# The squared norm of the second layer norm's vectors, from ScalarE row sums to TensorE column sums

## The reference, cut to what matters

```
x = mobius_add(residual, expmap0(attn_t))
residual = x
xn = layer_norm(logmap0(x))
xm = expmap0(xn * (1 + sc_mlp) + sh_mlp)
ff = plin(plin(xm, w_f1, b_f1), w_f2, b_f2)      # plin(x,w,b) = expmap0(logmap0(x) @ w + b)
```

## Time and profile before

| what | value |
|---|---|
| median of 3 runs | 459.88 us (459.84 to 459.92) |
| the profiled execution: its own time | 458.45 us |
| the profiled execution: span from first to last instruction | 456.3 us |
| TensorE busy | 371.9 us, 81% of the span |
| VectorE busy | 302.3 us, 66% |
| ScalarE busy | 231.8 us, 51% |
| GpSimd busy | 75.1 us, 16% |
| mean granted TensorE clock | 0.938 of full speed |

### The profile page before, as it was taken

How to read it: one execution, slowest core, us unless ns; L and a number is a source line. 1 busy time by engine, 2 the same in 40 slices (tenths; PEclk the granted TensorE clock), 3 DMA queues, 4 the chain that set the end, 5 groups by cost and what they waited for, 6 DMA issues and landing times.

```text
span 456.3 us, 14117 instructions
## 1 busy us (share of the span) xinstructions
PE 371.9 (81%) x5296; PEld 252.8 (55%) x5296; DVE 302.3 (66%) x1938; ACT 231.8 (51%) x1026; POOL 75.1 (16%) x149
## 2 busy tenths in 40 slices
PE   3998999798758897857998999979599889868833
PEld 2655675576646665646666766636344446447411
DVE  5454444675878776787776776653832388699883
ACT  2224422225435324436446455645688888954952
POOL 4000000121000021000022000042200125265580
PEclk9999999999999999999999999985759999995966
DMA  6301910010000000000000000000000000000102
GB/s 177 67 2 38 210 37 1 2 41 11 1 1 3 3 2 1 2 2 1 2 3 3 1 4 1 2 2 4 1 2 3 1 3 3 1 2 1 24 1 69
DMA packets 9561, 8.42 MB, mean 18 GB/s; under 512 B 1275, under 2 KB 8205, under 8 KB 9494
## 3 DMA queue, kind: packets, MB, share of 16 engines
q1 hardware_dynamic: 8950, 7.26, 7.1%
q10 hardware_dynamic: 544, 0.26, 0.2%
HBM read 6.45 MB, written 1.08 MB: 16 GB/s over the span
## 4 chain that ended last, share of the span: by engine, by line
PE 55%; DVE 22%; ACT 12%; issue 5%; POOL 4%; DMA 1%; SPq 0%; DVEq 0%; ACTq 0%; POOLq 0%
PE zb L805 21%; PE tb L928 6%; PE zb L784 4%; DVE prod_hi L1575 4%; PE tb L751 3%; ACT state L1270 3%; PE firsts L1099 2%; PE firsts L984 2%; PE tb L899 2%; ACT prd L1427 2%; PE firsts L968 2%; ACT state L1273 2%; PE zb L790 2%; PE zb L1079 2%; PE firsts L805 1%
## 5 line engine op out<-in xcount | busy, mean ns | idle before, releaser
L805 PEld LDWEIGHTS zb<-prod_hi,whh 128*128 128x128 f16 x1920 | 73.5, 106 | 89.5 <-DVE prod_hi L1575 85.4
L1270 ACT ACTIVATE state<-zb 128x8 f32<-128x8 f32 x240 | 42.7, 178 | 151.9 <-PE zb L805 151.5
L805 PE MATMUL zb<-prod_hi,whh 128*128 128x8 f16 x1920 | 90.8, 171 | 34.4 <-DVE prod_hi L1575 33.7
L1575 DVE SCALAR_TENSOR_TENSOR prod_hi<-state 128x16 f16<-128x16 f32 x255 | 44.6, 175 | 81.9 <-ACT state L1273 79.0
L805 PE MATMUL zb<-prod_lo,whh 128*128 128x8 f16 x960 | 63.2, 172 | 0.0
L1581 DVE TENSOR_TENSOR prod_lo<-prod,prod_hi 128x16 f16<-128x16 f32 x255 | 44.7, 175 | 8.7
L1427 ACT ACTIVATE prd<-zb 128x640 f32<-128x640 f32 x64 | 42.0, 710 | 5.0 <-PE zb L1079 4.3
L805 PEld LDWEIGHTS zb<-prod_lo,whh 128*128 128x128 f16 x960 | 44.0, 106 | 0.9
L1577 DVE SCALAR_TENSOR_TENSOR prod<-state 128x16 f32<-128x16 f32 x256 | 43.2, 169 | 0.3 <-ACT state L1273 0.3
L1273 ACT ACTIVATE state<-zb 128x16 f32<-128x16 f32 x240 | 42.8, 178 | 0.0
L1583 DVE SCALAR_TENSOR_TENSOR state<-prod 128x8 f32<-128x8 f32 x256 | 40.8, 159 | 0.0
(11 more groups left out here) (377 smaller groups left out, 697.2 us busy)
## 6 DMA issues: line engine op xcount, KB each, us to landing
mod<-ada_rows SPq DMA_DIRECT2D x4, 768.0 KB, 11.4
resid<-in_x_dram SPq DMA_DIRECT2D x6, 128.0 KB, 2.9
ffz<-shift_rows SPq DMA_DIRECT2D x4, 131.0 KB, 3.2
out_dram<-state SPq DMA_DIRECT2D x8, 64.0 KB, 2.1
out_dram<-early SPq DMA_DIRECT2D x8, 64.0 KB, 2.1
yy<-in_L_cond_w_ada_dram SPq DMA_DIRECT2D x1, 384.0 KB
early<-in_L_cond_weight_dram SPq DMA_DIRECT2D x2, 128.0 KB
resid<-in_x_dram ACTq DMA_DIRECT2D x2, 128.0 KB, 3.4
```

The lines of the kernel that those rows point to most:

```text
L805: i = pe.matmul(z_bank(t, k)[:, NB * (t % CH):NB * (t % CH) + NB], whh[:, half, p, k, :], src[:, NB * p:NB * p + NB], start=False, stop=Fa ...
L1270: act.activation(r[:, 24:32], z_bank(t, 1)[:, k:k + NB], ACT.Tanh, scale=-1.0 / ZS)
L1575: dve.scalar_tensor_tensor(prod_hi[:, :], r[:, 16:32], 1.0, r[:, 0:16], ALU.add, ALU.mult).then_inc(hi_ready, 1)
```

## The change

The four row sums on ScalarE go. In their place ScalarE makes one square of the transposed copy `T_OT[j]` (128x512, into `T_F[j]`), and TensorE multiplies each 128x128 tile of it with two columns of ones (`ones2`): four more matmuls of 128x2, into two columns that were free in the bank of t6. They stand behind the g products, and `t6_ps` is raised only behind them. VectorE's copy takes four values instead of three for each tile; its first step of `usum` reads the norm from that copy and no longer waits for `v_sq`. `ones2` is filled once at the start.

```diff
--- before.py
+++ after.py
@@ -238,6 +238,7 @@
         b0h = sb("b0h", [1, 2, 2, D], F16)
         onesh = sb("onesh", [1, 512], F16)
         ones = sb("ones", [1, P])
+        ones2 = sb("ones2", [P, 2])
         identf = sb("identf", [P, P])
         identh = sb("identh", [P, P], F16)
         condr = sb("condr", [NB, D])
@@ -1194,9 +1195,13 @@
 
                             ins = pe.matmul(b[:, 8 * c:8 * c + LIN], T_OT[j][:, c, :], lin[:, j, :],
                                             start=(c == 0), stop=True, skip_group_check=True)
-                        ins.then_inc(t6_ps, 1)
                         yield from at_ticks(now, base + T["g"][p])
                         products(j, "g", T_OT[j], gw[:, 0:D]).then_inc(g_ps, 1)
+                        pe.wait_ge(v_sq, j + 1)
+                        for c in range(NC):
+                            ins = pe.matmul(b[:, 8 * c + LIN:8 * c + LIN + 2], T_F[j][:, c, :], ones2[:, :],
+                                            start=False, stop=True, skip_group_check=True)
+                        ins.then_inc(t6_ps, 1)
                     for p, j in enumerate(PAIRS[n]):
                         yield from at_ticks(now, base + T["gy"][p])
                         products(j, "gy", T_OT[j], gw[:, D:2 * D]).then_inc(gy_ps, 1)
@@ -1479,8 +1484,8 @@
                         act.wait_ge(vT_ps, j + 1)
                         act.activation(T_OT[j], of_bank(j, "vT"), ACT.Copy).then_inc(vT_sb, 1)
                         yield from at_ticks(now, base + T["vsq"][p])
-                        act.wait_ge(v_ready, j + 1)
-                        squares(j, T_F[j], T_O[j], lambda col: st("vsq", col), v_sq)
+                        act.wait_ge(vT_sb, j + 1)
+                        act.activation(T_F[j], T_OT[j], ACT.Square).then_inc(v_sq, 1)
                     for p, j in enumerate(pairs):
                         if j in (1, 2):
                             yield from at_ticks(now, base + T["b12s"][p])
@@ -1542,6 +1547,7 @@
 
 
             dve.memset(ones[:, :], 1.0)
+            dve.memset(ones2[:, :], 1.0)
             dve.memset(onesh[:, :], 1.0)
             dve.wait_ge(load_scan, 48)
             for k, off in ((0, D), (1, 0)):
@@ -2007,14 +2013,14 @@
                     settled(dve.scalar_tensor_tensor(var, ss, 1.0 / D, var, ALU.mult, ALU.subtract))
                     yield from artanh(now, base, T, cols, sel, "2", var, (v_norm, n + 1), v_a)
                     for p, j in enumerate(pairs):
-                        k = slot_of("lin", 3)
+                        k = slot_of("lin", 4)
                         yield from at_ticks(now, base + T["lin"][p])
                         dve.wait_ge(t6_ps, j + 1)
                         for half in range(2):
                             pp_ = slice(CH * half, CH * half + CH)
                             ins = dve.tensor_copy(
-                                view(stat[pp_, k, NC * j:NC * j + 1], [NT, 3], [2, 2], [1, 2]),
-                                view(tail_bank(j, "t6")[pp_, half:half + 1], [2, 3], [16, 2],
+                                view(stat[pp_, k, NC * j:NC * j + 1], [NT, 4], [2, 2], [1, 2]),
+                                view(tail_bank(j, "t6")[pp_, half:half + 1], [2, 4], [16, 2],
                                      [9 - 2 * half, 2]))
                         ins.then_inc(v_lin, 1)
                         yield from at_ticks(now, base + T["gdot"][p])
@@ -2023,14 +2029,13 @@
 
                     yield from at_ticks(now, base + T["usum"])
                     dve.wait_ge(v_rho, n + 1)
-                    dve.wait_ge(v_sq, pairs[-1] + 1)
                     dve.wait_ge(v_lin, pairs[-1] + 1)
                     if n == 0:
                         dve.wait_ge(zsh_in, 64)
                     rho = st("rho2", sel)
-                    vsh, vG, vt = (stat[:, k + i, sel] for i in range(3))
+                    vsh, vG, vt, vsq = (stat[:, k + i, sel] for i in range(4))
                     u, q, t = st("usq2", sel), tmp[:, 23, cols], tmp[:, 24, cols]
-                    done_(dve.tensor_tensor(u, st("vsq", sel), rho, ALU.mult))
+                    done_(dve.tensor_tensor(u, vsq, rho, ALU.mult))
                     mark = done[0]
                     yield from part(now, base, T, "usum", 0)
                     settle(mark)
```

## The result

The changed kernel takes 464.59, 462.93 and 463.64 us in three runs, against 459.84 to 460.29 us of the kernel before, measured beside it: ratio 1.0088 (1.0065 to 1.0112), +4.0 us (3.0 to 5.2). Six more runs in a second comparison gave 1.0071 (1.0050 to 1.0092), +3.3 us. The prediction was 462.1, +2.25 us, with a range up to 463.6: the sign was right, the size too small by 1 to 1.8 us.

A forecast was written before the change was run, and what follows sets the result against it. No engine bounds the whole span; only the stretch from 374 us on counts, by which queue passes delay on. Terms 1.2 + 0.2 + 0 + 0.85 = 2.25 us on 459.88 gave 462.1 us, range 460.3 to 463.6.

The forecast's parts named there:

- Eight passes: TensorE's four added float32 matmuls of 128x2 in each tail: 0.85 us at full clock, 1.6 at half clock.
- Tail 0: VectorE's copy waits for the ones behind g, so gdot and the last value products come 1.2 us later (0.7 to 1.4).
- Tail 1: The ones delay tail 2's output projection, which has 0.66 us slack before VectorE reads it: 0.2 us (0 to 0.43).
- Tail 2: Passes at half clock end before VectorE's copy is due; TensorE's idle 0.72 us makes good the late transposes: cost 0.
- Tail 3: Ones between g and gy delay f2sum, read with 0.04 us slack, then a serial chain: 0.85 us (0.37 to 1.09).
- ScalarE's relief: One square for four saves about 0.57 us of ScalarE per tail, but off the path: taken at 0.
- The signs named for "right": Tail 0's gdot 1.2 us later, passes about 0.1 us apart, and f2sum with tail 1's product 0.8 later against g.
- rival (c): Shorter TensorE idle before 411.06 us shifts the clock's fall or return: no gain, or 3 to 5 us more; chance 0.06.
- TensorE works without a gap there: At tail 0's squares TensorE has no idle time, so ScalarE's shorter square gets it no earlier.
- a free-running beat: The clock gate checks activity on a beat no matmul starts, so the clock's return may shift between runs.
- Tail 0's hand-over: At 390.67 us VectorE's 1.2 us delay passes through the save of O to TensorE's last value products, 0.1 us behind.
- inside it: In tail 0, TensorE's own 0.85 us delay is contained in VectorE's 1.2 us, not added on top.

The follow-up runs named there:

- fill: Kernel before plus only VectorE's fill of ones2 in the start: +0.5 us (-0.3 to +1.2).
- relief: Kernel before with ScalarE's four row-sum squares per tail replaced by one square without sums, that computation left out: 460.42 us, 0.0 us.
- late fills: GpSimd's first fills of V and O released by VectorE's cast prod_hi: 460.09 us on the kernel before, 463.50 us on the changed kernel.
- fill free: Late fills, with TensorE's wait for the last fill moved to the first scores: 457.31 us on the kernel before, 461.86 us on the changed kernel.
- passes at t6: Changed kernel with the ones products directly behind the linear terms, ahead of g: 462.86 us; with the fill free edits too, 459.48 us.
- the pause: Kernel before with four small VectorE products ahead of gdot in tail 0 and no pass added: 468.07 us, +8.2 us.
- changed again: The changed kernel unaltered, run once more for a second profile: 463.65 us, +3.3 us against the kernel before.
- passes only: Kernel before with four 128x2 products per tail added on TensorE ahead of g, ScalarE and VectorE as before: 463.11 us, +3.1 us.
- tail 0 alone: Kernel before with the four 128x2 products added in tail 0 only: 462.35 us, +1.8 us.
- gdot ahead of the copy: Changed kernel with VectorE's gdot ahead of its copy of the four terms: 463.97 us, +5.7 us.

## Why the prediction was too low

**Terms that held.** Eight passes: 0.88 us for 0.85. Tail 0: 1.17 for 1.2. Tail 1: 0.18 for 0.2. Tail 2: 0. Tail 3: 0.87 for 0.85. ScalarE's relief: 0.0 in a kernel of its own. Together 2.22 for 2.25. The signs named for "right" are there: gdot 1.19 later, passes 0.11 us apart, f2sum 0.87 later against g.

**The step that failed: the clock.** The sum gave it nothing, and rival (c), with a chance of 0.06, looked for it in one place, the return in tails 2 and 3, and set it at 3 to 5 us. What came is smaller, and mostly elsewhere. In six profiles with the tails of before (two of before, fill, relief, late fills, fill free) the clock had no stretch at 0.50 from 376 us to the end of the sum for x2 of tail 2 (1.02 us from 406.33 on in before); five of them had one that ended between 370 and 376, at a cost of 0.5 to 1.1, so the count is only of what is added behind that. With passes just ahead of g or behind it there was one in eight of nine (the ninth is the one with the idle time filled); with the passes at t6 in none of two. With the changed kernel's passes behind g the loss from the value products to vT of tail 1 was 0.66, 0.01, 1.73 and 1.74 us. By the whole tail, four profiles of the changed kernel (two as it is, late fills, fill free) lose 3.4, 3.7, 5.0 and 3.9 us behind 361, mean 4.0; the six with before's tails 0, 1.1, 1.4, 0.8, 1.4 and 0.5, mean 0.9. The difference, 3.1 to 3.2 us, is 2.2 of terms and 0.9 of clock. By the same means of four and six profiles the 0.9 is 1.0 more between the value products and vT of tail 1 and 0.15 more in tail 1, less 0.3 ahead of g of tail 0, where the added passes don't stand yet; from vT of tail 2 on it is nothing (0.35 against 0.3, the passes' 0.87 taken off). The runs say 3.3 and 4.0, and 3.0 and 4.7 with late fills. The half microsecond that is left of their mean is inside the intervals.

I had read "TensorE works without a gap there" up to 389 us and 1.18 us idle behind it, and asked only what a delay does to the next start, not what it does to the clock of everything behind.

**How the fall comes about** is open. That a pass isn't always needed: shown by the pause, in one profile. That filling the idle time takes the fall away: not shown; one profile has none with fillers, and one has none without. That it saves time: no. That idle time is needed: no; in three of the eight profiles with the added fall (changed again, passes only, tail 0 alone) it came 0.4 to 0.8 us behind passes, with TensorE busy up to it. The prediction cited the Trainium skill, "TensorE: Matmul & The Clock Gate", "What's actually happening", for a free-running beat and for a moment of the return that may shift between runs. The shift is now there: in the second execution of the kernel before, TensorE's work at the return ahead of tail 3 stood 1.9 us later and the return only 1.0 (421.5 against 420.5), and that execution has a fall at 363.5 us that the first doesn't have. A beat itself no run shows.

**Tail 0's hand-over** had its size and its place right: the save of O ends at 394.43 and the value products start at 394.53, the 0.1 us of the forecast. But the copy ahead of gdot is not the only way in which VectorE gets late. Without it, VectorE waits for TensorE's late value products, and 0.84 of the 1.17 remains. The forecast had TensorE's own delay "inside it", which fits.

**Open.** Why 1.30 us of delay in tail 0 cost 8.2, in executions that no profile caught; why gdot ahead of the copy, which lost less in its profile, was no faster; and what sets the moment of a fall. The late return ahead of tail 3, which the first profile seemed to add, is not the change's: from vT of tail 2 to the last residual sum, changed kernels lost 1.45, 1.68, 0.90 and 0.85 us, the passes' 0.87 included, and those with before's tails 0, 0, 0.84, 0.17, 0.82 and 0.

## What to carry to other kernels

Price added work or a delay twice: once as time handed on, and once for a stretch of TensorE that may run at 1.2 GHz behind it, with idle time ahead of the fall or without; here the second part was 0.9 us on 2.2 by the mean of the profiles, and anything from 0 to 1.7 at one place. Four small float32 products are no small thing (0.88 us, nearly what four full 128-column ones take, 1.09); put them into an existing idle time, ahead of a wait (1.22 us in all in the profiles, clock included), not behind the product that others wait for (2.2, and 0.9 of clock). A clock held high is worth nothing while another engine sets the pace, so look at who is waited for before filling gaps.

## What was not expected of the hardware

A cast of 128x16 took 0.17, 2.10 or 3.47 us, by whether and for which of GpSimd's fills it had to wait. The same program's scan differed by 0.3% from run to run (1.0781 against 1.0816 us a step between the 32nd and the 64th). Moving the fills behind the cast alone gave nothing; with the wait behind them moved too it gave 2.4 us.
